# A fused attention and expert layer: in each head's slot but one, the probability transposes stand ahead of the next batch's projection pieces

## The chip, the cores and the metric

The kernel runs on one core of a Trainium2 chip. The metric is the device time of one execution in microseconds (us). Three timed runs of the kernel before took 1635.76, 1637.66 and 1641.44 us; the median is 1637.66 us. One further execution was profiled.

## What is computed

There are 32 batches. Each has 112 query rows of width 256 and 375 context rows of width 256 with a mask, and there are 8 heads of width 64. Cut to what matters, and leaving out the layer norms' formulas:

```python
kv  = concat(layernorm(context) * gamma + beta, layernorm(x) * kv_gate)   # 375 + 112 rows
q, k, v = latents @ Wq, kv @ Wk, kv @ Wv                                  # per head 64 wide
sim  = q k^T * SCALE, masked
attn = softmax(sim)
x1   = x + tanh(g0) * (concat_heads(attn @ v) @ Wout)
# then a mixture of 8 experts, 2 chosen per row:
out  = x1 + tanh(g1) * sum_e combine[e] * (silu(z @ gate_e) * (z @ up_e)) @ down_e,   z = layernorm(x1)
```

The change touches the order of work in the attention stage alone.

## The kernel before

The program has two stages, one after the other. The first, up to some 940 us of the profiled span, does attention and routing for the 32 batches; the second runs 63 tiles of 128 routed rows through the experts. Each engine (TensorE, VectorE, ScalarE, GpSimd, SyncE) has its own written-out instruction list, and the lists are kept in step by semaphores alone. In each list the function `body(b, p)` does one batch's turn; bodies 2 to 27 run in a hardware loop of 13 rounds with one even and one odd body each, the others are written out. An engine works its list strictly in the order written.

A body has eight slots, one for each head h. It is a software pipeline over three batches:

- `sims` (even slots, for heads h and h+1): q k^T into the two banks simP. It waits (line 1247) until VectorE's `masked_max` (line 858) has read both banks.
- `masked_max` on VectorE adds the mask and finds the row's maximum; `exps` on ScalarE (line 656) makes the probabilities pr.
- `probs_T(b, h-2)` on TensorE (line 1261): four transposes of pr into the bank ptP of that head's parity. It waits for `exps` of its head and for the eviction of the head two before.
- ScalarE (`probs_hi`, line 663) and then VectorE (`probs_lo`, line 864) evict ptP into pT as a high and a low f16 half.
- `values(b, h-3)` on TensorE (line 1272, instructions under line 1203, oP): twelve matmuls of pT by v. For head 0 it waits until VectorE's `heads_out` (line 876, tile ao) has emptied oP of the batch before.
- `piece(b+1, ., n)` on TensorE (instructions under line 1203, fP): one part of the next batch's projections. PQ, PQ+1 in slot 0 give q; PK to PK+3 (two in slot 2, one each in slots 3 and 4) give k; PV to PV+3 (slots 4 to 7) give v. There are two banks fP, so a piece waits until the piece two before it is evicted, first by ScalarE (`piece_hi`, line 649, the high half) and then by VectorE (`piece_lo`, line 848, the low half).
- In slot 1 `rows_T` transposes rows of batch b+2 through the same banks fP. Slot 4 has `heads_T` (line 1279, tile ao into tP), slot 5 `out_proj` (instructions under line 1203, tP), which needs VectorE's `heads_out_lo` (line 881, aoT); slot 7 has `norm2_T` (line 1290), which needs VectorE's z (line 902). Slot 5 of odd bodies has `ranks` (lines 1305 to 1309), which writes a corner of a ptP bank.

ScalarE's slot is: pieces' high halves, `probs_hi(h-2)`, `exps(h)`. VectorE's slot is: `heads_out` of the last batch (slot 3), `masked_max(h)`, pieces' low halves, `heads_out_lo` (slot 4), `norm2` (slot 6), `probs_lo(h-2)`, then the residual (slot 5), statistics (slot 3) and, in odd bodies, the routing's small operations in between. Both lists stand as they are in the changed kernel.

TensorE's body as it is, with what calls it and what it calls:

Of the kernel before, what the change touches and what calls it, by code (L numbers as in the profile page):

```python
# [15 lines left out]
B, S, D = 32, 112, 256  # L16
# [3 lines left out]
H, DH = 8, 64  # L20
# [44 lines left out]
def build(nc, x, ctxt, mask, scal, lnw, wqkv, wout, confw, confbw, wffn, out):  # L65
# [4 lines left out]
    with ctx:  # L70
# [194 lines left out]
        def need(eng, semaphore, count):  # L265

            if not isinstance(count, int) or count > 0:
                eng.wait_ge(semaphore, count)
# [5 lines left out]
        def holds(b, lo, hi):  # L274

            return lo <= b <= hi if isinstance(b, int) else True
# [7 lines left out]
        def zseq(b, k):  # L284

            return k if isinstance(b, int) and b == 0 else seq(b - 2, PZ + k)
# [909 lines left out]
        def _(pe):  # L1196
# [12 lines left out]
            def bank_free(number):  # L1209

                need(pe, s_phi, number - 1)
                need(pe, s_plo, number - 1)

            def rows_T(b):
                pe.wait_ge(s_z, b + 1)
                for k in range(KD):
                    bank_free(zseq(b, k))
                    for i in range(CJ):
                        nc.tensor.transpose(fP[k][:, i * CP:(i + 1) * CP], z[0:CP, i, k * P:(k + 1) * P], ident[0:CP, 0:CP])
                    nc.tensor.transpose(fP[k][:, SC:SC + S], z[0:S, 3, k * P:(k + 1) * P], ident[0:S, 0:S]).then_inc(s_piece, 1)  # L1220

            def piece(b, p, n):

                if n == PQ:
                    pe.wait_ge(s_zsplit, b + 1)
                bank_free(seq(b - 1, n))
                o = fP[n % 2]
                if n < PZ:
                    for m in range(QB):
                        c = (n * QB + m) * P  # L1230
                        last = product(o[:, m * S:(m + 1) * S], lambda k, a: weight(0)[:, a, k, c:c + P],
                                       lambda k, a: zTs[p][:, a, k, QC:QC + S], KD)
                elif n < PV_:
                    m = n - PK
                    last = product(o[:, 0:NK], lambda k, a: weight(1)[:, a, k, m * P:(m + 1) * P],
                                   lambda k, a: zTs[p][:, a, k, 0:NK], KD)
                else:
                    c = n - PV_
                    last = product(o[:, 0:INNER], lambda k, a: zTs[p][:, a, k, c * KR:c * KR + P],
                                   lambda k, a: weight(2)[:, a, k, :], KD)  # L1240
                last.then_inc(s_piece, 1)

            def sims(b, p, h):

                n = b * H + h
                pe.wait_ge(s_plo, seq(b - 1, PK + h // 2) + 1)
                need(pe, s_max, n)
                for t, (a, c) in enumerate(PARTS):
                    for i in range(2):
                        r = slice(i * DH, (i + 1) * DH)  # L1250
                        last = nc.tensor.matmul(simP[i][:, 0:NK], qT[p][r, a, h // 2, :], kT[p][r, c, h // 2, :],  # L1251
                                                start=t == 0, stop=t == len(PARTS) - 1)
                        if t == len(PARTS) - 1:
                            last.then_inc(s_sim, 1)

            def probs_T(b, h):
                n = b * H + h
                pe.wait_ge(s_exp, n + 1)
                need(pe, s_ptlo, n - 1)
                for c in range(KC):  # L1260
                    last = nc.tensor.transpose(ptP[h % 2][0:KR, c, 0:S], pr[h % 2][:, c * KR:(c + 1) * KR], ident[0:S, 0:S])  # L1261
                last.then_inc(s_pt, 1)

            def values(b, p, h):
                n = b * H + h
                pe.wait_ge(s_ptlo, n + 1)
                if h == 0:

                    pe.wait_ge(s_plo, seq(b - 1, NPIECE))
                    need(pe, s_ao, b)  # L1270
                product(oP[:, h * DH:(h + 1) * DH], lambda k, a: pT[h % 2][:, a, k, :],
                        lambda k, a: v[p][:, a, k, h * DH:(h + 1) * DH], KC).then_inc(s_pv, 1)

            def heads_T(b):
                pe.wait_ge(s_ao, b + 1)

                need(pe, s_z2c, b)
                for m in range(MB):
                    last = nc.tensor.transpose(aoT_P[:, m, :], ao[:, m * P:(m + 1) * P], ident[0:S, 0:S])
                last.then_inc(s_aot, 1)  # L1280

            def out_proj(b):
                pe.wait_ge(s_aolo, b + 1)
                wo = ws[:, :, 3, :].rearrange("p h (m d) -> p h m d", m=MB)
                product(y_P, lambda k, a: aoT[:, a, k, :], lambda k, a: wo[:, a, k, :], MB).then_inc(s_y, 1)

            def norm2_T(b, p):
                pe.wait_ge(s_z2, b + 1)
                for k in range(KD):
                    last = nc.tensor.transpose(z2T_P[:, k, :], z2[p][:, k * P:(k + 1) * P], ident[0:S, 0:S])  # L1290
                last.then_inc(s_z2t, 1)

            def confidences(b):
                pe.wait_ge(s_z2c, b + 1)
                need(pe, s_lg, b)
                for k in range(KD):
                    last = nc.tensor.matmul(lg_P, z2T[:, k, :], confT[:, k, :], start=k == 0, stop=k == KD - 1)
                last.then_inc(s_logit, 1)

            def ranks(b, pair):  # L1300


                pe.wait_ge(s_oh, pair + 1)
                pe.wait_ge(s_ptlo, b * H + 2 if holds(b, 0, B - 1) else B * H)
                nc.tensor.matmul(rank_P[:, 0:E], earlier[:, :], both[:, 0, :], start=True, stop=True)
                nc.tensor.matmul(rank_P[:, E:2 * E], earlier[:, :], both[:, 1, :], start=True, stop=False)
                nc.tensor.matmul(rank_P[:, E:2 * E], ones[0:S, 0:S], both[:, 0, :], start=False, stop=True)
                nc.tensor.matmul(tot_P, ones[0:S, 0:S], both[:, 0, :], start=True, stop=False)
                nc.tensor.matmul(tot_P, ones[0:S, 0:S], both[:, 1, :], start=False, stop=True).then_inc(s_rank, 1)

            def body(b, p, pair=None):
                for h in range(H):
                    if h % 2 == 0 and holds(b, 0, B - 1):
                        sims(b, p, h)
                    if h == 4 and holds(b, 1, B):
                        heads_T(b - 1)
                    if h == 1 and holds(b, 0, B - 3):
                        rows_T(b + 2)
                    if holds(b, 0, B - 2):
                        for n in SLOT_PIECES.get(h, []):  # L1320
                            piece(b + 1, 1 - p, n)
                    if h == 5 and holds(b, 1, B):
                        out_proj(b - 1)
                    if h == 7 and holds(b, 1, B):
                        norm2_T(b - 1, 1 - p)
                    if h < 2 and holds(b, 1, B):
                        probs_T(b - 1, H - 2 + h)
                    if h == 5 and p == 1 and holds(b, 3, B + 1):
                        ranks(b, (b - 3) // 2 if isinstance(b, int) else pair)
                    if h >= 2 and holds(b, 0, B - 1):  # L1330
                        probs_T(b, h - 2)
                    if h < 3 and holds(b, 1, B):
                        values(b - 1, 1 - p, H - 3 + h)
                    if h >= 3 and holds(b, 0, B - 1):
                        values(b, p, h - 3)
                    if h == 0 and holds(b, 2, B + 1):
                        confidences(b - 2)
# [8 lines left out]
            for n in range(NPIECE):  # L1346
                if n == PZ:
                    rows_T(1)
                elif n != PZ + 1:
                    if n == PV_:  # L1350
                        pe.wait_ge(s_wready, 2)
                    piece(0, 0, n)
            body(0, 0)
            body(1, 1)
            with pe.Fori(1, PAIRS - 2) as j:
                body(j * 2, 0)
                body(j * 2 + 1, 1, j - 1)
# [122 lines left out]
```

## Time and profile before

| | |
|---|---|
| median of three timed runs | 1637.66 us |
| lowest, highest | 1635.76, 1641.44 us |
| span of the profiled execution | 1632.5 us |
| TensorE busy with matmuls, share of the span | 88% |
| VectorE, ScalarE, GpSimd busy | 58%, 52%, 37% |
| mean granted TensorE clock | 0.971 of 2.4 GHz |

The span runs from the first to the last instruction of the profiled execution. Its time outside the span is not recorded; the median of the timed runs is 5.1 us above the span. In the rows further down "start us, us" are the start after the span's begin and the time of a merged group of instructions, "x4" is their number, and a bracket at the end gives the engine's idle time just before and what released it. An engine's name stands ahead of the line number in kernel.py: PE is TensorE's matmul side, PEld its weight loads, DVE VectorE, ACT ScalarE.

### The profile page before, as it was taken

To read this page: it belongs to the slowest core of one execution; us is meant where nothing else is said; L and a number is where in the kernel's file an instruction comes from. 1 tells how busy PE (TensorE), PEld (TensorE's weight loads), DVE (VectorE), ACT (ScalarE), POOL (GpSimd) and SP (SyncE) were. 2 spreads that over 40 slices of the span, in tenths; PEclk is the share of its full clock that TensorE was granted. 3 is DMA by queue.
4 is the path that set the end of the run, shared out by engine and by line. 5 is a ranking of instruction groups with operands and counts; after the bars stand their busy time and mean duration, and the time that the engine had idled before them with its cause. 6 is when DMAs were issued, how large, how long until landed. Compare 5 with 4: busy or idle time off the path is not lost.

```text
span 1632.5 us, 39655 instructions
## 1 busy us (share of the span) xinstructions
PE 1429.1 (88%) x11944; PEld 1084.8 (66%) x11945; DVE 953.5 (58%) x2651; ACT 843.4 (52%) x1873; POOL 599.9 (37%) x666
## 2 busy tenths in 40 slices
PE   0599989998999899989998659999999999999956
PEld 0266656665666565656565447888888778888845
DVE  3388888888888888888887634233332223333311
ACT  3377777777777777777776422223332223333311
POOL 3244544654465446543653321222222222222211
PEclk9899999999999999999999869999999999999987
DMA  3124234423342344233423387411113771111183
GB/s 97 49 78 153 92 107 135 162 91 108 133 162 91 110 132 162 91 111 130 162 79 110 142 262 220 132 29 26 29 26 82 239 220 26 29 26 29 26 256 82
DMA packets 70907, 180.57 MB, mean 111 GB/s; under 512 B 11664, under 2 KB 33552, under 8 KB 70864
## 3 DMA queue, kind: packets, MB, share of 16 engines
q1 hardware_dynamic: 54464, 153.66, 28.2%
q0 software_dynamic: 15264, 24.25, 7.6%
q10 hardware_dynamic: 1136, 2.12, 0.5%
q8 instruction: 23, 0.38, 0.1%
q14 instruction: 20, 0.16, 0.0%
HBM read 106.91 MB, written 73.09 MB: 110 GB/s over the span
## 4 chain that ended last, share of the span: by engine, by line
PE 63%; DVE 13%; issue 9%; DMA 8%; ACT 2%; POOL 1%; another core or an unknown queue 1%; SPq 1%; DVEq 1%; POOLq 0%; ACTq 0%
PE fP L1203 15%; PE yP L1203 10%; PE gP L1203 9%; PE uP L1203 9%; PE simP L1251 4%; DMA W<-split_experts 4%; PE ptP L1261 3%; PE oP L1203 3%; PE aP L1387 3%; PE tP L1203 3%; DMA out<-ysb,xt 2%; DVE pT L864 2%; DMA xt<-routed_rows 1%; DVE ms L858 1%
## 5 line engine op out<-in xcount | busy, mean ns | idle before, releaser
L1142 DVE TENSOR_TENSOR act_h<-uP,sg 128x512 f32<-128x512 f32 x126 | 87.1, 691 | 290.4 <-ACT sg L756 290.4
L1203 PE MATMUL fP<-zTs,ws 128*128 128x112 f16 (+1 forms) x1536 | 220.6, 294 | 25.6 <-DVE kT L848 13.0
L1203 PE MATMUL gP<-W,xT 128*128 (+1 forms) x756 | 212.2, 417 | 33.3 <-issue 26.1
L756 ACT ACTIVATE sg<-gP 128x512 f32<-128x512 f32 x126 | 75.4, 598 | 290.8 <-PE uP L1203 289.0
L858 DVE CUSTOM_DVE_ANT_0 ms<-simP,madd,sim_undo 112x488 f32<-112x488 f32 x256 | 184.7, 722 | 37.1 <-remote 19.8
L557 POOL DMA_INDIRECT out<-ysb,xt x63 | 100.6, 1597 | 271.7 <-ACT ysb L768 256.3
L1203 PEld LDWEIGHTS yP<-W,aT 128*128 128x128 f32 x1512 | 191.1, 193 | 10.1 <-issue 5.3
L1203 PE MATMUL yP<-W,aT 128*128 (+1 forms) x1512 | 192.9, 284 | 4.7 <-DVE aT L1146 4.7
L1203 PE MATMUL uP<-W,xT 128*128 (+1 forms) x756 | 196.0, 395 | 0.0
L1203 PE MATMUL fP<-ws,zTs 128*128 128x512 f16 x768 | 186.9, 379 | 10.3 <-DVE kT L848 10.1
L656 ACT ACTIVATE pr<-ms,nmax 112x488 f32<-112x488 f32 x256 | 179.2, 700 | 31.4 <-DVE nmax L858 27.6
L1203 PEld LDWEIGHTS fP<-zTs,ws 128*128 128x128 f16 x1536 | 109.8, 99 | 118.1 <-issue 33.9
L1146 DVE TENSOR_TENSOR aT<-aP,aT 128x512 fp32r<-128x512 f32 x126 | 86.5, 686 | 163.3 <-ACT aT L762 163.3
L1203 PEld LDWEIGHTS gP<-W,xT 128*128 128x128 f32 x756 | 136.8, 194 | 59.9 <-issue 37.4
L663 ACT ACTIVATE pT<-ptP 122x448 f16<-122x448 f32 x256 | 138.1, 539 | 72.7 <-PE ptP L1261 70.5
L864 DVE SCALAR_TENSOR_TENSOR pT<-ptP,pT 122x448 f16<-122x448 f32 x256 | 158.2, 618 | 25.1 <-ACT pT L663 16.7
L1203 PEld LDWEIGHTS uP<-W,xT 128*128 128x128 f32 x756 | 144.8, 191 | 32.1
L762 ACT ACTIVATE aT<-aP 128x512 fp32r<-128x512 f32 x126 | 75.1, 596 | 170.8 <-PE aP L1387 170.8
L1203 PE MATMUL oP<-v,pT 122*128 122x64 f16 x3072 | 133.2, 194 | 20.7 <-DVE ao L876 19.6
L1261 PE MATMUL ptP<-ident,pr 112*122 112x112 f32 x1024 | 143.1, 262 | 0.0
L1203 PEld LDWEIGHTS oP<-v,pT 122*128 122x128 f16 x3072 | 123.3, 98 | 26.6 <-issue 17.0
L1261 PEld LDWEIGHTS ptP<-ident,pr 112*122 112x122 f32 x1024 | 115.8, 141 | 25.0 <-ACT pr L656 1.2
(204 smaller groups left out, 2261.3 us busy)
## 6 DMA issues: line engine op xcount, KB each, us to landing
split_experts<-wparts SPq DMA_DIRECT2D x32, 1536.0 KB, 6.6
W<-split_experts SPq DMA_DIRECT2D x64, 768.0 KB
wr<-wffn SPq DMA_DIRECT2D x32, 768.0 KB, 8.0
xc<-ctxt SPq DMA_DIRECT2D x32, 375.0 KB
xt<-routed_rows POOLq DMA_DIRECT2D x63, 129.0 KB, 2.4
xl<-x SPq DMA_DIRECT2D x32, 112.0 KB
xres<-x SPq DMA_DIRECT2D x32, 112.0 KB, 7.8
out<-x SPq DMA_DIRECT2D x32, 112.0 KB, 1.9
```

Of the source, the lines that this page charges most:

```text
L557: pool.indirect_dma_start(out[:, :], bass.IndirectOffsetOnAxis(ap=xt[k][:, D:D + 1].bitcast(I32), axis=0), ysb[k % 2][:, :], None, compute ...
L656: nc.scalar.activation(pr[h % 2][:, :], ms[h % 2][:, :], ACT.Exp, bias=nmax[p][:, h:h + 1], scale=-1.0, accum_out=rsum[p][:, h:h + 1]).the ...
L663: nc.scalar.activation(pT[h % 2][:, 0, :, 0:S], ptP[h % 2][0:KR, :, 0:S], ACT.Copy, scale=P_TOP).then_inc(s_pthi, 1)
L756: nc.scalar.activation(sg[i][:, :], gP[i][:, :], ACT.Silu).then_inc(s_silu, 1)
L762: nc.scalar.activation(aT[q][i][:, 0, :, :], aP[i][:, :, :], ACT.Copy).then_inc(s_athi, 1)
L858: nc.vector.tensor_tensor_reduce(out=ms[h % 2][:, :], in0=simP[h % 2][0:S, 0:NK], in1=madd[p][:, :], scale=sim_undo[0:S, 0:1], scalar=3.0e ...
L864: nc.vector.scalar_tensor_tensor(out=pT[h % 2][:, 1, :, 0:S], in0=ptP[h % 2][0:KR, :, 0:S], scalar=P_TOP, in1=pT[h % 2][:, 0, :, 0:S], op0 ...
L1142: nc.vector.tensor_tensor(act_h[i][:, :], uP[i][:, :], sg[i][:, :], ALU.mult).then_inc(s_act, 1)
L1146: nc.vector.tensor_tensor(aT[q][i][:, 1, :, :], aP[i][:, :, :], aT[q][i][:, 0, :, :].bitcast(F32), ALU.subtract).then_inc(s_atlo, 1)
L1203: last = nc.tensor.matmul(o, lhs(k, a), rhs(k, c), start=n == 0, stop=n == len(todo) - 1)
L1251: last = nc.tensor.matmul(simP[i][:, 0:NK], qT[p][r, a, h // 2, :], kT[p][r, c, h // 2, :], start=t == 0, stop=t == len(PARTS) - 1)
L1261: last = nc.tensor.transpose(ptP[h % 2][0:KR, c, 0:S], pr[h % 2][:, c * KR:(c + 1) * KR], ident[0:S, 0:S])
```

## The change

The choice of which head is transposed in a slot becomes a function `probs_of`, with the same conditions as before. In every slot but slot 5 it is called ahead of the pieces; in slot 5 it stays where it was, behind `out_proj` and `ranks`. Nothing else changes: the same instructions run on every engine, and only TensorE's order differs. In slot 1 there are no pieces, so the order is as it was (`rows_T`, then the transposes). In slot 7 the transposes also pass `norm2_T`.

```diff
+            def probs_of(b, h):
+
+                if h < 2 and holds(b, 1, B):
+                    probs_T(b - 1, H - 2 + h)
+                if h >= 2 and holds(b, 0, B - 1):
+                    probs_T(b, h - 2)
+
             def body(b, p, pair=None):
                 for h in range(H):
                     if h % 2 == 0 and holds(b, 0, B - 1):
@@ -1316,6 +1323,8 @@
                         heads_T(b - 1)
                     if h == 1 and holds(b, 0, B - 3):
                         rows_T(b + 2)
+                    if h != 5:
+                        probs_of(b, h)
                     if holds(b, 0, B - 2):
                         for n in SLOT_PIECES.get(h, []):
                             piece(b + 1, 1 - p, n)
@@ -1323,12 +1332,10 @@
                         out_proj(b - 1)
                     if h == 7 and holds(b, 1, B):
                         norm2_T(b - 1, 1 - p)
-                    if h < 2 and holds(b, 1, B):
-                        probs_T(b - 1, H - 2 + h)
                     if h == 5 and p == 1 and holds(b, 3, B + 1):
                         ranks(b, (b - 3) // 2 if isinstance(b, int) else pair)
-                    if h >= 2 and holds(b, 0, B - 1):
-                        probs_T(b, h - 2)
+                    if h == 5:
+                        probs_of(b, h)
                     if h < 3 and holds(b, 1, B):
                         values(b - 1, 1 - p, H - 3 + h)
                     if h >= 3 and holds(b, 0, B - 1):
```

## Rows read from the trace of the kernel before

**Rows 1.** Busy us (instructions) of PE, PEld, DVE, ACT, POOL; clock, DMA share, GB/s.

```profile
200.00:900.00 700.00, 641.34 (x6670) 429.66 (x6669) 592.87 (x1804) 514.58 (x1177) 360.10 (x396) 1.00 0.36 122
```

**Rows 2.** Waits, 200 to 900 us: waiter, releaser, total us, times, longest us.

```profile
ACT pT L663 <- PE ptP L1261: 51.8, 38, 2.2
...
PE fP L1203 <- DVE kT L848: 21.1, 25, 1.4
...
PE simP L1251 <- DVE nmax L858: 15.4, 14, 1.3
...
PE oP L1203 <- DVE ao L876: 13.0, 13, 1.1
...
PEld tP L1203 <- DVE aoT L881: 5.6, 14, 0.4
```

**Rows 3.** Timeline of an odd body, from slot 2's second piece to slot 4.

```profile
480.29 0.55 PE L1261 MATMUL ptP<-ident,pr 112*122 112x112 f32 x4
...
480.49 0.58 ACT L649 ACTIVATE kT<-fP 128x488 f16<-128x488 f32 x1 [0.46 <-PE fP L1203]
...
480.68 0.52 PE L1203 MATMUL oP<-v,pT 122*128 122x64 f16 x12
...
481.10 0.67 DVE L848 SCALAR_TENSOR_TENSOR kT<-fP,kT 128x488 f16<-128x488 f32 x1 [0.37 <-ACT kT L649]
...
482.98 0.68 DVE L876 TENSOR_TENSOR ao<-oP,rinv 112x512 f32<-112x512 f32 x1
...
483.81 0.51 PE L1203 MATMUL oP<-v,pT 122*128 122x64 f16 x12 [0.99 <-DVE ao L876]
...
484.37 0.79 PE L1251 MATMUL simP<-kT,qT 64*128 64x488 f16 x6
```

**Rows 4.** Timeline of an even body, slot 4 to the start of `out_proj`.

```profile
514.09 0.60 PE L1279 MATMUL tP<-ident,ao 112*128 112x112 f32 x4
...
514.53 1.40 PE L1203 MATMUL fP<-zTs,ws 128*128 128x488 f16 x6
...
517.26 0.60 ACT L649 ACTIVATE v<-fP 122x512 f16<-122x512 f32 x1 [0.72 <-PE fP L1203]
...
517.89 0.69 DVE L848 SCALAR_TENSOR_TENSOR v<-fP,v 122x512 f16<-122x512 f32 x1 [0.24 <-ACT v L649]
...
518.50 0.61 DVE L881 SCALAR_TENSOR_TENSOR aoT<-tP,aoT 128x448 f16<-128x448 f32 x1
...
519.17 1.52 PE L1203 MATMUL tP<-ws,aoT 128*112 128x256 f16 x12
```

**Rows 5.** Timeline of the even body's slots 6 and 7, to the next `sims`.

```profile
523.38 0.55 PE L1261 MATMUL ptP<-ident,pr 112*122 112x112 f32 x4
...
523.83 0.58 ACT L649 ACTIVATE v<-fP 122x512 f16<-122x512 f32 x1
...
524.44 0.69 DVE L848 SCALAR_TENSOR_TENSOR v<-fP,v 122x512 f16<-122x512 f32 x1
...
525.90 0.72 DVE L858 CUSTOM_DVE_ANT_0 ms<-simP,madd,sim_undo 112x488 f32<-112x488 f32 x1
...
526.68 0.79 PE L1251 MATMUL simP<-kT,qT 64*128 64x488 f16 x6
```

**Rows 6.** Timeline of body 30's slot 7, after the loop.

```profile
910.03 0.50 PE L1290 MATMUL tP<-ident,z 112*128 112x112 f32 x2 [4.85 <-DVE z L902]
910.33 0.95 PE L1261 MATMUL ptP<-ident,pr 112*122 112x112 f32 x4
911.07 0.85 PE L1203 MATMUL oP<-v,pT 122*128 122x64 f16 x12
```

**Rows 7.** Timeline of the even body's slots 3 and 4.

```profile
511.11 1.40 PE L1203 MATMUL fP<-zTs,ws 128*128 128x488 f16 x6 [0.84 <-DVE kT L848]
...
512.58 0.72 DVE L858 CUSTOM_DVE_ANT_0 ms<-simP,madd,sim_undo 112x488 f32<-112x488 f32 x1
...
513.37 0.79 PE L1251 MATMUL simP<-kT,qT 64*128 64x488 f16 x6
```

## The prediction

> **What bounds the kernel now.** I read the busy time by stretch first. From 200 to 900 us, where the hardware loop lies, TensorE is busy 641.34 of 700 us, VectorE 592.87, ScalarE 514.58, and the granted clock is 1.00, that is the 2.4 GHz level [rows 1]. TensorE looks like the bound, but 59 us of it are idle, and that idle time has to be somewhere. So the list of waits came second. TensorE waits for four things, each 13 or 14 times (the loop has 13 rounds of an even and an odd body), or 25: for fP's eviction (21.1 us), for the maxima (15.4 us), for ao (13.0 us) and, on the weight-load side, for aoT (5.6 us) [rows 2]. A wait that comes once a round with nearly the same length is no accident but a link of a chain. The reader should see there that every one of these releasers is VectorE. The third view, the timeline of one even and one odd body, shows who released VectorE in turn, and there it is twice TensorE's own piece: TensorE finishes a piece, ScalarE has been waiting for it, VectorE has been waiting for ScalarE, and TensorE then waits for VectorE. The bound is this loop through three engines, not TensorE's work. The change moves one part of it.
>
> What one move is worth: four transposes stand 0.39 us ahead of what follows (480.29 to 480.68) [rows 3]. Behind another kind of matmul and ahead of a piece, the four similar transposes of `heads_T` take 0.44 us (514.09 to 514.53) [rows 4]. So every piece behind moved transposes ends 0.39 to 0.44 us later, counted from its slot's start, and `values`, last in the slot, starts where it did.
>
> **Step 1, the supposed gain: ptP earlier.** ScalarE waits 51.8 us for the transposes, but in only 38 waits for 206 heads [rows 2]. ScalarE's list has the pieces' high halves ahead of `probs_hi` in every slot, and this order isn't changed. In the slots that change, ScalarE first waits for the piece, copies it (0.58 us [rows 3]), and the transposes behind it (0.39 us) are long done. The long waits belong to slot 5 (`out_proj` and `ranks` stand between), which isn't touched, and to slot 1, which has no pieces. I put the gain at 0. From both sides: it can't be under 0, as the transposes only come earlier; were it the whole 0.39 us in the six changed slots of 28 bodies it would be 65 us, which needs ScalarE waiting for ptP there, and it waits for fP.
>
> **Step 2, odd body, slots 2 to 4: a loss.** The second k piece ends just as `probs_T` begins at 480.29. ScalarE had been idle 0.46 us for that piece and copies it at 480.49; VectorE had been idle 0.37 us for ScalarE and starts at 481.10; it then works through without a pause to ao at 482.98; TensorE waits 0.99 us for ao and starts `values` of head 0 at 483.81, and `sims` at 484.37 stands behind it and the next maximum [rows 3]. With the transposes ahead of both pieces each of these comes 0.39 to 0.44 us later. No link has slack, since each engine was already waiting. TensorE does `probs_T(1)` of slot 3 ahead of its piece, but this lies inside the wait for ao. I take 0.42. It happens in the odd bodies 1 to 29, 15 times: 6.3 us. Below it is 0, if VectorE catches up later; the row at 0.37 speaks against that, since what VectorE does next is the work TensorE waits for.
>
> **Step 3, even body, slots 4 and 5: a loss.** ScalarE waited 0.72 us for the first v piece, until 517.26, and VectorE 0.24 us for ScalarE. VectorE does v, then aoT from 518.50 to 519.11, and `out_proj` starts at 519.17 [rows 4]: 0.06 us behind its releaser. The list of waits has its weight load waiting for aoT 14 times [rows 2]. The piece comes 0.39 us later (its transposes now follow `heads_T`, so the lower price), and so does `out_proj`. TensorE has no other work there: `values(1)` and the next piece are placed as before. Behind it TensorE works to the end of the body with next to no idle time, so nothing takes the loss back. Bodies 2 to 28, 14 times 0.39: 5.5 us. Body 30 has 4.85 us of idle time in its slot 7 [rows 6] and can hide it.
>
> **Step 4, even body, slot 6: a small loss.** The v piece ends close to 523.55 (the transposes start at 523.38 beside its tail). ScalarE copies it only at 523.83, without idle time, so it has some 0.25 us of slack with the signal's 0.06. A piece 0.44 us later leaves 0.2 us. VectorE's low half at 524.44 follows it at once, and from there VectorE's chain to the maximum at 525.90 and `sims` at 526.68, 0.06 us behind the maximum's end, has no pause [rows 5]. 14 times 0.2: 2.8 us. The bounds are 0 and 0.44 each.
>
> **Step 5, what is hidden.** Slot 0: the q pieces come 0.4 us later. In odd bodies ScalarE and VectorE follow by that much, and the maximum of head 1 then ends about when TensorE comes to `sims(2)`: 0, at most 0.1. In even bodies VectorE is behind with the odd body's routing operations and doesn't notice: 0. Slot 3, even: the transposes fill part of TensorE's 0.84 us wait for kT [rows 7]; rival B is about this. Slots 6 and 7, odd: TensorE waits at the end of the body for the maximum anyway, 15.4 us in 14 times [rows 2]: 0. No DMA or queue of SyncE or GpSimd is passed, and their semaphores come as late as the rest and no later. Slot 7: the transposes pass `norm2_T`. In the loop that is worth less than 0.1. In body 30 it waits 4.85 us for z, and the transposes behind it take 0.74 us at the lower clock, 910.33 to 911.07 [rows 6]; now they are done in the wait: 0.7 us gained, once.
>
> By the Trainium skill, "TensorE: Matmul & The Clock Gate", section "LDWEIGHTS (loading the stationary operand)", a load of 122 columns would take some 102 ns, and loads hide behind running matmuls; by an estimate from it, transposes that now follow `values` in slot 7, whose 64-column matmuls hide little, cost about 0.1 us more. Nothing above rests on that.
>
> **Sum.** 6.3 + 5.5 + 2.8 - 0.7 = 13.9 us on the profiled execution's 1632.5 us of span, so 1646.4 us. What lies around the span is taken from the runs shown, whose median is 5.1 us above it: 1651.5 us, 0.85% over the median. With step 4 at its ends the case runs from 11.1 to 17.3, with step 2 at 0.39 or 0.44 half a us around that, and the untouched first bodies may add or take 2: its own range is 1647 to 1657 us.
>
> **Rivals.**
>
> A, no change: 1637.7 us. TensorE's work is the same to the instruction, and it is the busiest engine; if it is the bound, order is worth nothing. Steps 2 and 3 would then be absorbed by the idle time of 59 us. For it: TensorE is 92% busy [rows 1]. Against it: the idle time is not spread but sits right behind VectorE's links. The Trainium skill has this rival as a rule, "Perfetto Trace Analysis", section "Identifying the Most-Contended Engine": the engine with the highest occupancy is the one that counts (with a reservation on TensorE's matmul busy time); by it alone the time would stay.
>
> B, faster: 1631.8 us. In the even body's slot 3 TensorE stands 0.84 us for kT [rows 7]. The transposes, 0.39 us, now fit in that wait, so that `values` and all behind could come 0.39 us earlier, 15 times: 5.9 us. It decides if TensorE and not VectorE is last at `sims(4)`. Against it: VectorE's maximum from 512.58 ends at 513.30, and `sims` starts at 513.37 [rows 7]; this does not move. It also needs steps 2 and 3 to be absorbed.
>
> C, dearer: 1660 us. Links that now just hold (the k eviction ahead of slot 5's piece, the maximum ahead of `sims(2)`) slip too, by 0.3 us in each of the 28 bodies: 8.4 us more than the sum. For it: several ends lie within 0.1 us of their use. Against it: each was worked to 0.1 or less.
>
> **Chances.** My forecast 0.74, A 0.10, B 0.07, C 0.09. The range of 1640 to 1662 us leaves out A, B and a little of the forecast's edges. A measurement of this kernel can tell about 0.3%, or 4.9 us, from no change. C and all but 0.03 of the forecast are slower by more than that: slower 0.80; same is A and these 0.03, 0.13; faster is B, 0.07.
>
> **What would show it.** Right: two bodies take about 1.0 us longer than before, the wait for ao in the odd body starts in the same slot and `values(0)` comes 0.4 us later after `sims(2)`, `out_proj` in even bodies shows a wait for aoT of about 0.4 us, the wait for kT in even slot 3 shrinks by 0.39 us and one for ao or the maximum takes its place. TensorE's busy time stays, its idle time from 200 to 900 us grows. Wrong: if TensorE has no new wait for aoT, step 3 fails; if ScalarE's waits for ptP in the loop fall much below 51.8 us, step 1; if `sims` follows the maximum in even slot 7 as before and the body is no longer, step 4.

## The result, and the profile after

The changed kernel took 1652.16 us, the median of four runs (1651.45 to 1655.03); the kernel before took 1636.71 us in the four beside it. The ratio is 1.0109, with a 95% interval of 1.0082 to 1.0136. The profiled executions have spans of 1650.0 and 1632.5 us, at the same mean clock of 0.971. The forecast was 1651.5 us for the timed runs and 1646.4 us for the span. The text ahead of the prediction puts 5.1 us around the span. That figure compares two different executions and is too large: wherever a run's time and its own span are both on record, the time is 1.5 to 2.2 us above the span, and 1.7 us in the profiled run of the changed kernel.

The page of the kernel after shows nearly the same busy times as before, with fewer per cent of a longer span:

```profile
PE 1436.7 (87%) x11944; PEld 1081.4 (66%) x11945; DVE 954.1 (58%) x2651; ACT 843.0 (51%) x1873; POOL 598.9 (36%) x666
```

The busy time of the same stretch as in [rows 1] (columns as there), after:

```profile
200.00:900.00 700.00, 634.52 (x6528) 419.68 (x6526) 582.26 (x1771) 507.21 (x1161) 351.91 (x392) 1.00 0.35 119
```

Every engine did less in the same 700 us: TensorE 634.52 instead of 641.34 us, so its idle time grew from 58.7 to 65.5 us, at an unchanged clock of 1.00. The instructions are the same and there are more holes between them. The list of waits of the kernel after (waiter, releaser, total us, times, longest us; 200 to 900 us, as in [rows 2]) shows where:

```profile
ACT pT L663 <- PE ptP L1261: 55.3, 36, 2.5
...
PE fP L1203 <- DVE kT L848: 18.8, 24, 0.9
PE oP L1203 <- DVE ao L876: 17.9, 25, 1.1
...
PE simP L1251 <- DVE nmax L858: 15.4, 13, 1.3
...
PEld tP L1203 <- DVE aoT L881: 10.2, 13, 0.8
...
PE tP L1203 <- DVE aoT L881: 3.8, 13, 0.3
```

The last line is new: before, only the weight load waited for aoT (5.6 us); now it waits 10.2 us and the matmuls wait too. The wait for ao now comes 25 times instead of 13, that is in even bodies as well. ScalarE's wait for the transposes did not shrink (51.8 us before). What grew in it is the wait in slot 5 of the even body, from 1.22 to 1.60 us in each round: its transposes still stand behind `out_proj`, which now starts later.

The place of the loss can be read more sharply by cutting each body at the starts of `sims`. Medians over the loop's 13 rounds, in us, worked out from the timelines:

| slots | even 0-1 | 2-3 | 4-5 | 6-7 | odd 0-1 | 2-3 | 4-5 | 6-7 | two bodies |
|---|---|---|---|---|---|---|---|---|---|
| before | 5.46 | 7.21 | 7.99 | 5.33 | 4.76 | 7.28 | 9.74 | 6.61 | 54.37 |
| after | 5.46 | 7.65 | 8.37 | 5.53 | 4.79 | 7.44 | 9.74 | 6.67 | 55.66 |
| difference | 0 | 0.44 | 0.38 | 0.20 | 0.03 | 0.16 | 0 | 0.06 | 1.29 |

The loop took 16.4 us more (705.8 to 722.2), the two bodies ahead of it 2.4, the four behind it 1.2, together 20.0 us. The rest of the span, nearly all of it work in which no order was changed, came out 2.6 us shorter in this pair of profiles. These sum to 17.5 (rounded), the difference of the spans.

The odd body of the kernel after, from slot 2 to slot 4, answers to [rows 3] (timeline: start us, us, then the instruction, and in brackets the engine's idle time before it and the releaser):

```profile
546.52 2.47 POOL L456 TENSOR_TENSOR zTs<-zT,zTs 128x1200 f16<-128x1200 f32 x1 [2.18 <-ACT zTs L637]
...
547.53 0.58 ACT L649 ACTIVATE kT<-fP 128x488 f16<-128x488 f32 x1 [0.66 <-PE fP L1203]
...
548.14 0.67 DVE L848 SCALAR_TENSOR_TENSOR kT<-fP,kT 128x488 f16<-128x488 f32 x1 [0.57 <-ACT kT L649]
...
548.72 0.30 DVE L932 TENSOR_TENSOR bids<-bids,confb 112x16 f32<-112x16 f32 x1
...
549.75 0.68 DVE L876 TENSOR_TENSOR ao<-oP,rinv 112x512 f32<-112x512 f32 x1
...
550.58 0.51 PE L1203 MATMUL oP<-v,pT 122*128 122x64 f16 x12 [1.09 <-DVE ao L876]
```

The waits of ScalarE and VectorE each grew by 0.20 (0.46 to 0.66, 0.37 to 0.57). The start of bids (548.72) matters later. The even body of the kernel after, slots 2 to 7, answers to [rows 7], [rows 4] and [rows 5] in turn:

```profile
577.62 1.24 DVE L848 SCALAR_TENSOR_TENSOR kT<-fP,kT 128x488 f16<-128x488 f32 x2 [0.25 <-ACT kT L649]
...
578.43 1.40 PE L1203 MATMUL fP<-zTs,ws 128*128 128x488 f16 x6 [0.77 <-DVE kT L848]
...
579.90 0.71 DVE L858 CUSTOM_DVE_ANT_0 ms<-simP,madd,sim_undo 112x488 f32<-112x488 f32 x1
...
580.13 0.51 PE L1203 MATMUL oP<-v,pT 122*128 122x64 f16 x12 [0.30 <-DVE ao L876]
...
580.68 0.79 PE L1251 MATMUL simP<-kT,qT 64*128 64x488 f16 x6
...
581.85 0.55 PE L1261 MATMUL ptP<-ident,pr 112*122 112x112 f32 x4
...
582.23 1.40 PE L1203 MATMUL fP<-zTs,ws 128*128 128x488 f16 x6
...
584.96 0.60 ACT L649 ACTIVATE v<-fP 122x512 f16<-122x512 f32 x1 [0.72 <-PE fP L1203]
...
585.59 0.69 DVE L848 SCALAR_TENSOR_TENSOR v<-fP,v 122x512 f16<-122x512 f32 x1 [0.62 <-ACT v L649]
...
586.20 0.61 DVE L881 SCALAR_TENSOR_TENSOR aoT<-tP,aoT 128x448 f16<-128x448 f32 x1
...
586.87 1.52 PE L1203 MATMUL tP<-ws,aoT 128*112 128x256 f16 x12 [0.29 <-DVE aoT L881]
...
592.34 0.69 DVE L848 SCALAR_TENSOR_TENSOR v<-fP,v 122x512 f16<-122x512 f32 x1 [0.27 <-ACT v L649]
...
594.58 0.79 PE L1251 MATMUL simP<-kT,qT 64*128 64x488 f16 x6
```

In slot 3 the wait for kT is 0.77 instead of 0.84, although the transposes now stand in it, and a new wait for ao (0.30) stands ahead of `values`. In slot 4 the transposes take 0.38 us ahead of the piece (581.85 to 582.23), VectorE's wait for ScalarE went from 0.24 to 0.62, exactly 0.38 more, and `out_proj` waits for aoT. In slot 6 VectorE's low half, which ran without idle time in [rows 5], now waits 0.27.

Body 30's slot 7, after, answers to [rows 6]:

```profile
930.14 0.41 PE L1290 MATMUL tP<-ident,z 112*128 112x112 f32 x2 [3.88 <-DVE z L902]
930.68 0.82 PE L1203 MATMUL oP<-v,pT 122*128 122x64 f16 x12
```

`values` follows 0.54 us behind `norm2_T` instead of 1.04 us: the transposes are done inside the wait, as forecast, for a gain of 0.5 us, once.

### The profile page after: what moved, and what is told of

It is laid out like the page before. It is cut to its first block, busy times and chain, and to the rows that moved or that the text cites. A ratio compares the mean times of both kernels' runs of the same rounds, so it can differ in the third digit from the quotient of the medians.

```text
span 1650.0 us, 39655 instructions
## 1 busy us (share of the span) xinstructions
PE 1436.7 (87%) x11944; PEld 1081.4 (66%) x11945; DVE 954.1 (58%) x2651; ACT 843.0 (51%) x1873; POOL 598.9 (36%) x666
## 4 chain that ended last, share of the span: by engine, by line
PE 57%; DVE 15%; issue 11%; DMA 8%; ACT 5%; POOL 1%; DVEq 1%; SPq 1%; POOLq 0%; another core or an unknown queue 0%; ACTq 0%
PE yP L1203 10%; PE fP L1203 9%; PE gP L1203 9%; PE uP L1203 9%; PE ptP L1261 4%; PE simP L1251 4%; DMA W<-split_experts 4%; PE aP L1394 3%; PE tP L1203 3%; DVE pT L864 2%; DMA out<-ysb,xt 2%; PE oP L1203 2%; DVE ms L858 2%; PE fP L1219 1%; DMA xt<-routed_rows 1%
## 5 line engine op out<-in xcount | busy, mean ns | idle before, releaser
L1203 PEld LDWEIGHTS fP<-zTs,ws 128*128 128x128 f16 x1536 | 115.6, 99 | 92.3 <-issue 15.6
L1261 PE MATMUL ptP<-ident,pr 112*122 112x112 f32 x1024 | 149.5, 269 | 0.0
L1261 PEld LDWEIGHTS ptP<-ident,pr 112*122 112x122 f32 x1024 | 105.6, 141 | 40.0 <-issue 37.2
```

Source lines behind the costliest of these rows:

```text
L1203: last = nc.tensor.matmul(o, lhs(k, a), rhs(k, c), start=n == 0, stop=n == len(todo) - 1)
```

## The experiments

Twelve kernels ran, in three sets, each beside the kernel before. Each set ran on another chip. The median of the kernel before was 1626.58 us in the first set (e1 to e4), 1637.05 us in the second (e5 to e8) and 1627.25 us in the third (e9 to e12); e5 and e10 have one run each, so no ratio is given for them. Sets 1 and 3 differ from the others in one segment: where slot 2 has the original order, the even body's slots 2-3 take 6.51 us in them, and 7.2 to 7.3 in set 2 and in the first comparison. The last heading comes back to this. The segments of every run, made as above (in e9 and e12 the even slots 0-1 vary from round to round between 6.0 and 8.9 us):

| us | even 0-1 | 2-3 | 4-5 | 6-7 | odd 0-1 | 2-3 | 4-5 | 6-7 | two bodies |
|---|---|---|---|---|---|---|---|---|---|
| e1 slot 2 | 5.46 | 6.94 | 7.99 | 5.33 | 4.76 | 7.31 | 9.74 | 6.61 | 54.13 |
| e2 slot 4 | 5.47 | 6.51 | 8.37 | 5.33 | 4.76 | 7.27 | 9.74 | 6.61 | 54.05 |
| e3 slot 6 | 5.47 | 6.51 | 7.99 | 5.53 | 4.76 | 7.27 | 9.74 | 6.68 | 53.94 |
| e4 slot 0 | 5.46 | 6.51 | 7.99 | 5.33 | 4.79 | 7.44 | 9.74 | 6.61 | 53.87 |
| e5 before | 5.46 | 7.32 | 7.99 | 5.33 | 4.76 | 7.28 | 9.74 | 6.61 | 54.49 |
| e6 after | 5.46 | 7.73 | 8.37 | 5.53 | 4.79 | 7.45 | 9.74 | 6.68 | 55.75 |
| e7 before, bids later | 5.47 | 7.32 | 7.99 | 5.33 | 4.76 | 7.04 | 9.74 | 6.61 | 54.25 |
| e8 after, bids later | 5.47 | 7.73 | 8.37 | 5.53 | 4.79 | 7.47 | 9.74 | 6.68 | 55.77 |
| e9 before, split first | 7.11 | 6.51 | 7.99 | 6.17 | 4.76 | 7.27 | 9.74 | 10.81 | 60.39 |
| e10 slot 0 | 5.46 | 6.51 | 7.99 | 5.34 | 4.79 | 7.44 | 9.74 | 6.60 | 53.88 |
| e11 after, aoT early | 5.46 | 6.94 | 7.87 | 5.53 | 4.79 | 7.44 | 9.74 | 6.67 | 54.44 |
| e12 combination | 7.03 | 6.51 | 7.87 | 6.27 | 4.76 | 7.04 | 9.74 | 10.81 | 60.16 |

**e1 to e4: one slot at a time.** Each kernel is the changed one with the transposes ahead of the pieces in a single slot (shown for slot 2; the others have 4, 6 and 0 in its place):

```diff
-                    if h != 5:
+                    if h in (2,):
                         probs_of(b, h)
...
-                    if h == 5:
+                    if h not in (2,):
                         probs_of(b, h)
```

> The transposes stand ahead of the pieces in slot 2 alone; every other slot is as before. Theory V, the prediction's step 2 as written: the second k piece ends 0.43 us later, nothing between it and ao has slack, so the odd body is 0.42 us longer and the kernel 6.3 us slower than before. Theory G: VectorE's bids operation (line 932) stands between them, took 0.56 us before and 0.30 us after, and each time ended when GpSimd's zTs subtraction ended; it is released by GpSimd and not by the k eviction, so 0.1 us or less is lost in the odd body. The even body loses 0.03 us. By theory G two bodies take 54.4 to 54.5 us (before 54.36) and the kernel is 0 to 1.5 us slower.

Measured: 1633.05 us, ratio 1.0034 (1.0016 to 1.0052). The odd body's slots 2-3 took 7.31 us, 0.03 or 0.04 more than where slot 2 is untouched, not 0.4. The even body's took 6.94 instead of 6.51, where I had forecast 0.03 us more. The time alone would have misled here: the kernel became 6.5 us slower, which is what theory V forecasts, but the loss lies in the body for which theory V says nothing. The odd body bears out theory G.

> The transposes stand ahead of the pieces in slot 4 alone. Step 3 as written: out_proj of even bodies waits 0.3 to 0.4 us more for aoT, two bodies take 54.36 + 0.39 = 54.75 us, the kernel is 5.5 us slower. Rival: the v piece's delay is taken up elsewhere and two bodies stay at 54.36 us.

Measured: 1631.42 us, 1.0021 (1.0006 to 1.0036). Even slots 4-5 took 8.37 us instead of 7.99, and no other segment moved.

> The transposes stand ahead of the piece in slot 6 alone. Step 4 as written: two bodies take 54.36 + 0.20 = 54.56 us, all of it in the even body's slots 6 and 7; the kernel is 2.8 us slower. Rival: ScalarE's slack takes it up, no change.

Measured: 1632.18 us, 1.0028 (1.0010 to 1.0045). Even slots 6-7 took 5.53 us instead of 5.33, as forecast. Odd ones took 6.68 instead of 6.61, which neither the forecast nor its rival has.

> The transposes stand ahead of the q pieces in slot 0 alone. The prediction held this for free. Theory Q: it is the dearest slot. In the even body the signal of rows_T's second half, which ScalarE needs for zT, comes late (the 0.6 us wait of the changed kernel) and costs 0.4 us by slot 4; in the odd body ScalarE's zTs, and with it GpSimd's subtraction and the bids operation, come 0.16 us later. Two bodies then take 54.9 to 55.0 us and the kernel is 8 to 9 us slower. Rival, the prediction's step 5: 54.36 to 54.46 us, 0 to 1.5 us slower, and the even body's 0.46 us belong to slot 2 or 3.

Measured: 1628.86 us, 1.0017 (1.0000 to 1.0034). Odd slots 0-1 took 0.03 more and odd slots 2-3 took 7.44 instead of 7.28 or 7.27: the q pieces of slot 0 act in slots 2-3. So the odd half of theory Q holds, and its even half fails: the even slots 2-3 stayed at 6.51 us, and slot 0 is the cheapest of the four, not the dearest. The set has no late signals, so that the even half was not tried where they occur.

With the segments that no part touches as the base (53.68 us for two bodies, the sum of 5.46, 6.51, 7.99, 5.33, 4.76, 7.28, 9.74 and 6.61), the four slots cost 0.45, 0.37, 0.26 and 0.19 us. Their sum, 1.27, is the whole change's 1.29; the ratios' excesses sum to 1.00%, against 1.09%. So the parts add up, and slots 3 and 7, which had no run of their own, are left with next to nothing in the loop.

The same two links of the even slots 2-3 can be read in e1 and e4, whose `sims` of slot 2 start at 505.74 and 505.72. Timeline of e1, the second k piece's eviction and ao:

```profile
509.57 0.58 ACT L649 ACTIVATE kT<-fP 128x488 f16<-128x488 f32 x1 [0.66 <-PE fP L1203]
...
511.30 0.68 DVE L876 TENSOR_TENSOR ao<-oP,rinv 112x512 f32<-112x512 f32 x1
```

The same lines of e4, where slot 2 is as before:

```profile
509.12 0.58 ACT L649 ACTIVATE kT<-fP 128x488 f16<-128x488 f32 x1 [0.56 <-PE fP L1203]
...
510.84 0.68 DVE L876 TENSOR_TENSOR ao<-oP,rinv 112x512 f32<-112x512 f32 x1
```

Counted from the start of `sims`, the piece's eviction comes 0.43 us later in e1 (509.57 - 505.74 against 509.12 - 505.72), ao 0.44 us later, and `sims` of slot 4 as well: 6.94 - 6.51. This is the chain that step 2 described for the odd body, and the even body pays for it in full.

**e5 and e6: the two kernels again.** Unchanged, to have both profiles on one chip.

> The kernel before once more, for its profile on the chip of this set. In the profile of before ScalarE stood 0.86 us ahead of probs_hi in the even body's slot 1 and VectorE 1.2 us ahead of the maximum in slot 2; in three of the four kernels with one slot moved the even body's slots 2 and 3 (sims to sims) took 6.51 us instead of 7.21. Theory H: this is no matter of the kernel but of the execution or chip, so before itself takes 6.5 us there and 53.7 us for two bodies in some runs. Rival: the moves took it away, and before shows 7.21 and 54.37 us again.

Measured: one run of 1639.44 us. Seven of the eight segments repeat those of the first profile to 0.01 us; even slots 2-3 took 7.32 instead of 7.21. That is the rival's outcome on this chip. Theory H keeps some support from the other sets: there every kernel with slot 2 in the old order shows 6.51, and the kernel before is 10 us faster by its median, but it wasn't profiled there.

> The changed kernel once more, on the same chip as the profile of before of this set. If the costs of the single slots add up (slot 0: 0.20 us, slot 2: 0.47, slot 4: 0.38, slot 6: 0.27), two bodies take 1.3 us more than before on any chip, 55.0 us where before takes 53.7, and the kernel is 1.0 to 1.2% slower. Rival: a part of the 1.3 us belonged to the late signals of the first chip, and the loss is under 1 us for two bodies here.

Measured: 1655.88 us, 1.0113 (1.0093 to 1.0133). Two bodies took 1.26 us more than in e5, in the same segments as in the first comparison. The result repeats, and the rival (under 1 us) falls. The sum of the parts, 1.27 us from a set without late signals, holds in one that has them.

**e7 and e8: what hid the 0.42 us in the odd body.** The trace of the kernel before shows it when GpSimd's lines are read beside VectorE's, behind the kT of [rows 3]:

```profile
479.75 2.47 POOL L456 TENSOR_TENSOR zTs<-zT,zTs 128x1200 f16<-128x1200 f32 x1 [1.98 <-ACT zTs L637]
...
481.69 0.56 DVE L932 TENSOR_TENSOR bids<-bids,confb 112x16 f32<-112x16 f32 x1
```

GpSimd's subtraction ends at 482.22 and VectorE's bids, a product of 16 columns that takes 0.17 us in e7 and e8 below, ends at 482.25. It took 0.56 us in all 13 rounds. After the change it starts 0.42 us later, counted from `sims` of slot 2, and takes 0.30 us, while GpSimd's operation ends at 548.99 and bids at 549.02. Theory G: VectorE is held here until GpSimd is done, so a delay of what stands ahead of it costs nothing up to that point. The test moves bids behind GpSimd's operation, in both kernels:

```diff
-CHOOSE_AT = {2: (2, 2, 1), 3: (2, 2, 1), 4: (2, 1, 1)}
+CHOOSE_AT = {2: (2, 0, 3), 3: (2, 2, 1), 4: (2, 1, 1)}
```

(The three numbers are how many of the routing's small operations VectorE takes at three places of a slot; in slot 2 two of them move from the middle to the end.)

> The kernel before, with the second and third routing operation of slot 2 in VectorE's list moved behind probs_lo, so that the bids product no longer stands between the k eviction and probs_lo. Theory G (VectorE's bids product is held until GpSimd's zTs subtraction ends): it now comes when that subtraction has ended, takes 0.2 us instead of 0.56, and ao of odd bodies comes 0.2 to 0.3 us earlier: two bodies 0.2 to 0.3 us shorter, 3 to 4.5 us in all. Rival: the product itself takes 0.56 us in any place, no change.

Measured: 1635.26 us, 0.9983 (0.9962 to 1.0005). Odd slots 2-3 took 7.04 us instead of 7.28, and the rival falls: the product takes 0.17 us in its new place. The forecast of 3 to 4.5 us less in all is not shown by the time, whose interval takes in 1. Timeline of e7:

```profile
479.38 2.47 POOL L456 TENSOR_TENSOR zTs<-zT,zTs 128x1200 f16<-128x1200 f32 x1 [1.99 <-ACT zTs L637]
...
481.85 0.17 DVE L932 TENSOR_TENSOR bids<-bids,confb 112x16 f32<-112x16 f32 x1
...
483.21 0.51 PE L1203 MATMUL oP<-v,pT 122*128 122x64 f16 x12 [0.76 <-DVE ao L876]
```

> The changed kernel with the same move of the routing operations. Theory G: here the k eviction is late enough that the bids product waited for GpSimd for 0.1 us only, so this kernel gains 0 to 0.1 us in two bodies, and against the kernel before with the same move the odd body's slots 2 and 3 are 0.4 us longer, where with the operations in their old place it is 0.17. Rival: it gains as much as the other.

Measured: 1656.24 us, 1.0108 (1.0079 to 1.0137). Odd slots 2-3 took 7.47 us. Timeline of e8:

```profile
494.58 0.17 DVE L932 TENSOR_TENSOR bids<-bids,confb 112x16 f32<-112x16 f32 x1
...
495.93 0.51 PE L1203 MATMUL oP<-v,pT 122*128 122x64 f16 x12 [1.11 <-DVE ao L876]
```

With bids out of GpSimd's way it takes 0.17 us in both, and the change now costs 7.47 - 7.04 = 0.43 us in these slots, against 0.17 with bids where it was (7.45 - 7.28). That is the 0.42 of step 2, uncovered. Theory G holds. It also says where the 0.16 comes from that was left: from slot 0, whose later q pieces push ScalarE's zTs and so the start of GpSimd's subtraction. In e4, with slot 2 untouched, the subtraction starts 0.17 us later after `sims` of slot 2 than in the kernel before (2.83 against 2.66, medians), bids starts where it did (4.60) and is held 0.17 us longer. Timeline of e4:

```profile
479.29 2.47 POOL L456 TENSOR_TENSOR zTs<-zT,zTs 128x1200 f16<-128x1200 f32 x1 [2.18 <-ACT zTs L637]
...
481.06 0.73 DVE L932 TENSOR_TENSOR bids<-bids,confb 112x16 f32<-112x16 f32 x1
```

In e1, where slot 0 is untouched and bids comes late, it is free of the subtraction and takes 0.17 us:

```profile
481.65 0.17 DVE L932 TENSOR_TENSOR bids<-bids,confb 112x16 f32<-112x16 f32 x1
```

**e9: GpSimd's list in another order.** The indirect DMAs that GpSimd issues for the routed rows were moved behind its split of the expert weights, to see whether they are what delays signals in even slots 1 to 3 (theory S, last heading):

```diff
-                if p == 1 and holds(b, 3, B + 1):
-                    scatter((b - 3) // 2 if isinstance(b, int) else j - 1)
                 if holds(b, 0, B - 3):
                     need(pool, s_z2, b)
                     split_weights(b)
+                if p == 1 and holds(b, 3, B + 1):
+                    if holds(b, 0, B - 5):
+                        pool.wait_ge(s_zhi, b + 4)
+                    scatter((b - 3) // 2 if isinstance(b, int) else j - 1)
```

> The kernel before, with GpSimd's four indirect DMAs of an odd body moved behind its weight split and held until ScalarE has written zTs of the next body (slot 2), about 6 us later. Theory S: TensorE's signals come late in the even body's slots 1 and 2 because GpSimd issues these DMAs there; without them ScalarE's 0.86 us and VectorE's 1.2 us waits go and the even body's slots 2 and 3 take 6.5 us instead of 7.2 to 7.3, two bodies 53.7 instead of 54.4, 9 to 10 us in all; late signals may then show in slots 3 and 4. Rival: the late signals come from something else, the even body keeps its 7.2 to 7.3 us (or, on a chip that doesn't show them, 6.5 us with and without the move) and the time is the same.

Measured: 1714.00 us, 1.0536 (1.0506 to 1.0566). Two bodies took 60.39 us, 6.7 over the base. Even slots 2-3 took 6.51 us, but so they do in this set with the DMAs in their old place (e10), so that the run says nothing on theory S. What it does show is theory G on a larger scale. Timeline of e9 at the end of an odd body:

```profile
356.14 1.46 POOL L480 CAST wparts<-wr 128x1536 fp32r<-128x1536 f32 x1 [0.89 <-DVE z L904]
...
356.30 1.32 DVE L964 TENSOR_SCALAR w<-gexp 112x2 f32<-112x2 f32 x1
...
357.78 3.42 POOL L483 TENSOR_TENSOR wparts<-wr,wparts 128x1536 fp32r<-128x1536 f32 x1 [0.18 <-POOL wparts L480]
357.94 3.28 DVE L969 TENSOR_SCALAR wt<-w,gates 112x2 f32<-112x2 f32 x1
...
362.45 1.40 PE L1253 MATMUL simP<-kT,qT 64*128 64x488 f16 x6 [5.39 <-DVE nmax L860]
```

(Lines are numbered two higher here.) Two VectorE operations on two columns take 1.32 and 3.28 us, and end 0.02 us behind GpSimd's: 357.62 against 357.60, 361.22 against 361.20. In the kernel before they take 0.16 and 0.23 us, free of GpSimd. The excess is 4.21 us, and the odd slots 6-7 grew by 4.20 (10.81 against 6.61). The maximum stands behind them in VectorE's list, and `sims` waits 5.39 us. The other 2.5 us, in the even slots 0-1 and 6-7, were not traced to a cause. The mean granted clock also fell from 0.97 to 0.942, with TensorE idle for these stretches.

**e10: slot 0 again,** meant for a chip where even slots 2-3 take 7.2 us.

> The transposes ahead of the q pieces in slot 0 alone, as in the fourth run. Should this chip show the late signals (7.2 to 7.3 us for the even body's slots 2 and 3 in before): theory Q says that the changed kernel's other 0.4 us there come from slot 0, since the signal of rows_T is late before slot 2 begins, and this kernel shows 7.6 to 7.7 us. Rival: they come from slot 2's own order, and this one shows 7.2 to 7.3. Without late signals it says nothing new: 6.51 us.

Measured: one run of 1633.22 us; the segments are those of e4. Even slots 2-3 took 6.51 us here, so the run could not answer its question. It does repeat e4 on another chip.

**e11: taking step 3's wait away.** In the changed kernel VectorE's `heads_out_lo` (aoT) is moved ahead of the v piece in slot 4:

```diff
-                    if holds(b, 0, B - 2):
-                        for n in SLOT_PIECES.get(h, []):
+                    for i, n in enumerate(SLOT_PIECES.get(h, [])):
+                        if h == 4 and i == 1 and holds(b, 1, B):
+                            heads_out_lo(b - 1)
+                        if holds(b, 0, B - 2):
                             piece_lo(b + 1, 1 - p, n)
-                    if h == 4 and holds(b, 1, B):
-                        heads_out_lo(b - 1)
```

> The changed kernel, with VectorE's aoT eviction of slot 4 moved between the low halves of the slot's two pieces, ahead of the v piece's. Step 3's account (the v piece's delay reaches out_proj through VectorE's order alone): out_proj no longer waits, the even body's slots 4 and 5 take 8.0 us instead of 8.37, two bodies 55.3 instead of 55.7, 5 us in all. Rival: the next v piece or the maximum takes the place of that wait, and 8.37 stays.

Measured: 1640.26 us, 1.0086 (1.0052 to 1.0119). Even slots 4-5 took 7.87 us instead of 8.37, 0.12 less than in the kernel before. Timeline of e11:

```profile
521.84 0.61 DVE L881 SCALAR_TENSOR_TENSOR aoT<-tP,aoT 128x448 f16<-128x448 f32 x1
...
523.36 1.47 PE L1203 MATMUL tP<-ws,aoT 128*112 128x256 f16 x12
```

aoT is ready 0.9 us ahead of `out_proj`, which has no wait left, and the list of waits has no line for aoT on TensorE's sides. Step 3's route (piece, ScalarE, VectorE's v, aoT, `out_proj`) is the one that costs.

**e12: a version meant to be faster.** The kernel before with the transposes ahead of `norm2_T` in slot 7 alone, bids later as in e7, aoT early as in e11 and GpSimd's order of e9. The first, against the changed kernel:

```diff
-                    if h != 5:
+                    if h in (7,):
                         probs_of(b, h)
...
-                    if h == 5:
+                    if h not in (7,):
                         probs_of(b, h)
```

(and the three edits shown above).

> The kernel before with four things: the transposes ahead in slot 7 alone, the routing operations behind probs_lo in slot 2, aoT ahead of the v piece's low half in slot 4, and the later indirect DMAs. By the runs so far two bodies lose 0.24 us by the second and 0 to 0.1 by the third, 0.7 us once by the first; by theory S another 0.7 to 0.8 us for two bodies, 14 to 16 us faster than before in all, by its rival 4 to 5 us.

Measured: 1702.47 us, 1.0475 (1.0451 to 1.0500). The gains are there, 7.04 and 7.87 us in their segments, and e9's loss buries them. I had put e9's order in unmeasured, which was the mistake. No run shows a version faster than before: e7's interval reaches from 0.9962 to 1.0005. The three edits without GpSimd's order weren't run.

## Why the prediction was right, step by step

**What bounds the kernel: right.** TensorE's work is the same and it got more idle time, at the same clock; the chain through ScalarE and VectorE set the end. Rival A (no change) is out by the interval; the busiest engine, TensorE, was not the one whose load counted. The Trainium skill's rule in "Perfetto Trace Analysis", section "Identifying the Most-Contended Engine", is to optimize the engine with the highest occupancy first. Read as rival A read it, that the load of this engine alone counts, it gives no change, and the measured 1.0109 speaks against that reading; the page itself does not say that the order of an engine's work is free.

**Step 1: right.** ScalarE's waits for ptP came to 55.3 us, from 51.8 in [rows 2]. The transposes came earlier and nobody took them sooner. The 141 ns that the profile has for one of their loads of 122 columns (1024 loads, before and after) are more than the 102 ns of the prediction's side estimate, on which nothing rested.

**Step 2: the place was right, the size and the reason that it had no cover wrong.** Forecast 0.42 us in the odd body's slots 2-3, measured 0.16, of which slot 2 itself makes 0.03 or 0.04 (e1). "No link has slack, since each engine was already waiting" is the sentence that fails. It followed ScalarE, VectorE and TensorE and left GpSimd out; between kT at 481.10 and ao at 482.98 in [rows 3] stands bids, held to the end of GpSimd's subtraction. e7 and e8 show the 0.43 when the cover is taken off; e4 shows that the 0.16 belongs to slot 0.

**Step 3: right.** Forecast 0.39, measured 0.38 by the route described; e2 has it alone and e11 takes it away.

**Step 4: right.** Forecast 0.2, measured 0.20; e3 has it alone.

**Step 5: wrong in three places.** Slots 2-3 of the even body cost 0.44 us. The prediction has slot 3 among what is hidden and has no term for slot 2 at all: step 2 prices its two k pieces in the odd body alone, and no reason is given why the even body should be spared. The view of [rows 7] begins at slot 3; in the even body too ao and the maximum follow kT of slot 2 without idle time, and I checked only whether the transposes fit in the gap behind. Slot 0 was put at "0, at most 0.1" and costs 0.03 + 0.16; odd slots 6-7 were put at 0 and cost 0.06. Odd slot 4 was not priced either, and the odd slots 4-5 did cost nothing (9.74 in both). Body 30 gave 0.5 instead of 0.7.

**The sum.** 1.0 us was forecast for two bodies and 1.29 measured: by segments, 0.26 too much in odd slots 2-3, 0.44 + 0.03 + 0.06 too little in three that the sum has at nothing, and 0.01 wrong in steps 3 and 4 together (the rest is rounding). The first bodies the prediction calls "untouched", though the change acts in them too and step 2 counts body 1; otherwise no sum was made for them ("may add or take 2"). They lost 2.4 us, and the single runs show the same links there: 0.42 for slot 2 of body 1 (e1), 0.20 and 0.34 for slot 4 (e2), 0.40 and 0.43 for slot 6 (e3), 0.23 for slot 0 (e4). These make 2.0 of the 2.4. The sizes differ from the loop's, and no run was made to tell why; the slots 2-3 of body 0 vary by more than the effect among the runs with the same order in them (6.79 to 7.62 us). The total of 1651.5 against 1652.16 us is closer than the steps are, and that is luck. In the attention stage the profiles show a loss of 20.0 us where 13.9 was forecast. The rest of the span was 2.6 us shorter, and the span came out at 1650.0 us against the forecast 1646.4. The 5.1 us then added for what lies around the span, instead of 1.7, made up 3.4 of the missing 3.6.

**Rival B** fell, and more plainly than I had written: I expected the wait for kT to shrink by 0.39 us, and it shrank by 0.07, since kT itself came 0.4 us later; the wait for ao came on top. **Rival C** asked for 0.3 us a body more than the sum, which is 0.6 for two; measured were 0.28 more. A link that just held was there, in the even slots 2-3, but not one of those that it named: the maximum ahead of `sims(2)` gave 0.03, and no loss shows at the k eviction ahead of slot 5's piece (e11 brings slots 4-5 under their old time by moving aoT alone).

## What to carry to other kernels

When a filler is put ahead of the work that feeds a three-engine chain, the price is up to the filler's length at every consumer that was already waiting (0.44, 0.38 and 0.20 us here for a filler of 0.4), whatever the filler's own consumer gains; read it off the brackets of the next engine, one link at a time. Before writing "no slack" or "hidden", list the instructions of all engines in the stretch, the one off the path too: an instruction that takes longer than its twins and ends with another engine's is a cover, and up to its end an earlier delay is free. And cut the bodies at one repeated instruction: one such table of medians to 0.01 us told apart what timed runs of 0.2% each could not.

## What the hardware showed that I had not expected

**A VectorE operation can be held for the rest of a GpSimd one.** A product of 112x16 elements took 0.17 us free of GpSimd, and 0.56, 0.30 and 0.73 us (before, after, e4) beside a GpSimd subtraction of 2.47 us, and in all 13 rounds of each it ended 0.02 to 0.04 us behind that one. In e9 operations on 112x2 elements were held for 1.32 and 3.28 us. Others in the same stretch were not: bids has both inputs in SBUF, while kT (one input in PSUM) ran its usual 0.67 us beside the same subtraction. The Trainium skill says this in "SBUF — State Buffer", section "Who interferes with whom": a VectorE instruction with two SBUF inputs contends with a GpSimd instruction that reads SBUF, one with at most one SBUF input outside the two-port modes does not, and in a two-port mode, which `tensor_scalar` can enter, whichever of VectorE and GpSimd comes first has the shared port pair for its whole instruction while the other blocks. The traces agree as far as VectorE was the one held; that GpSimd is held in turn no run here shows (its subtraction took 2.45 to 2.48 us with bids beside it and without). Had I applied the rule to bids, step 2 would have come out near 0; slot 2 alone cost 0.03 or 0.04 us there (e1).

**What looks like late signals of TensorE, on some chips.** In the first comparison and in set 2 ScalarE stood waiting in even slot 1 for transposes that TensorE had finished. Timeline of the kernel before:

```profile
614.07 0.54 PE L1261 MATMUL ptP<-ident,pr 112*122 112x112 f32 x4
...
615.92 0.55 ACT L663 ACTIVATE pT<-ptP 122x448 f16<-122x448 f32 x1 [0.86 <-PE ptP L1261]
```

The matmuls end at 614.61 and ScalarE starts 1.31 us later, having waited 0.86. The instruction also waits until `values` of the head two before has read its tile, which ended at 612.26. In sets 1 and 3 it doesn't wait (timeline of e4):

```profile
504.89 0.54 PE L1261 MATMUL ptP<-ident,pr 112*122 112x112 f32 x4
...
505.78 0.54 ACT L663 ACTIVATE pT<-ptP 122x448 f16<-122x448 f32 x1
```

With this goes the 0.7 to 0.8 us of the even slots 2-3 (7.2 or 7.3 against 6.51). Over 14 even bodies that is some 10 us, about the difference between the medians of the kernel before in the sets (1637.05 against 1626.58 and 1627.25). Both kernels have it, so that it is not in the ratio, and it comes in the body in which GpSimd issues indirect DMAs. In e4 the same DMAs run at the same place (503.11 to 507.93 us, beside `sims` at 505.72) without any late signal, so that they alone are not the cause. What delays the signals stays open: e9 was to tell and met a chip without them. It also stays open whether the 0.44 us of these slots comes by slot 2 where signals are late, as they were in the comparison that the prediction was about. Where they aren't it does (e1), but in the profile after the late signals also reach ScalarE's copy of zT and with it the first k piece, so the same 0.44 may arrive there by another route.
